# Moving router steps of a mixture-of-experts layer by one unit and by two tiles, in a kernel whose order is written out by hand

## The chip, the cores and the metric

The kernel runs on one core of a Trainium2 chip. The metric is the device time of one execution in microseconds (us). A core has the engines PE (matrix products), DVE, ACT and POOL, and SP, which here issues nearly all plain transfers. Each engine works through its own instruction list in order; semaphores hold an instruction until another engine or a transfer has got to a given point.

## The reference, cut to what matters

The reference is a two-layer decoder on 1024 tokens of width 128. The change touches the feed-forward part of its first layer, a mixture of 8 experts of which each token uses 2, applied twice ("loops"):

```python
for _ in range(LOOPS):                                  # LOOPS = 2
    z_norm = rmsnorm(z, norm_w)
    scores = softmax(z_norm @ router_w)                 # 8 experts
    topk_vals, topk_idx = top_k(scores, 2)
    topk_vals = topk_vals / (sum(topk_vals) + 1e-9)
    mixed = sum over e of cw[:, e] * ((silu(z_norm @ w1[e]) * (z_norm @ w3[e])) @ w2[e])
    z = mixed
x = x + z
```

Then follows the second layer, whose first part is a scan over the tokens (a state space layer).

## The kernel before

The 1024 tokens are two halves of 512. Two loops over two halves make four passes, 0 to 3. Passes 0 and 3 are **dense**: for all 512 tokens every expert is computed, in 16 **units** (an expert's 256 hidden columns are two units). PE makes two products per unit (`unit_up`, L1331), ACT the silu (`unit_silu`, L1339), DVE the product of both (`unit_gated`, L1345). Every second unit PE multiplies back (`down`, L1373), and DVE adds the result, weighted by the tokens' shares, to the sum in XN (`mix`, L1790). In the last pass the units are called n = 0 to 15 here; `down` number m = 8 follows unit n = 3 and uses units 0 and 1, `down` 9 follows unit 5 and uses units 2 and 3, and so on. `down` m waits until `mix` m-1 has read the PSUM bank that both use.

Passes 1 and 2 are **sorted**: each token's two (token, expert) pairs get a slot in a list of 15 tiles of 128 rows that is sorted by expert. POOL scatters the rows to HBM by eight indirect DMAs (`sort_tokens`, L2590), SP loads the sorted list back (`load_sorted`, L2623). Tile i goes through PE's first product (`tile_up`, L1440), ACT's silu (L1566), DVE's product (`tile_gated`, L1833), PE's transposes (`turn_tile`, L1449), ACT's copy (`take_hidden`, L1573) and PE's second product (`tile_down`, L1462). DVE copies each pair of results (L1842), SP stores them (`store_answers`, L2630), and POOL gathers each token's two rows again by eight indirect DMAs (`gather_answers`, L2600). The tiles of both sorted passes run as one loop, i = 0 to 29, after the units of pass 0 and before those of pass 3. At the end of the first 15 tiles PE drains: the last tiles are turned and multiplied one after the other, without new tiles between them.

**A pass's router** is a chain over three engines. PE turns the normed tokens (`pass_turn`, L1232), ACT copies them with the norm's weight (`pass_scalar`, L1512), PE multiplies by the router (`pass_logits`, L1238). DVE takes the logits and subtracts their maximum (`pass_shift`, L1660 to L1663), ranks each token's experts (`pass_rank`, L1672 to L1681), ACT takes the exponent (`pass_gates`, L1517), and DVE makes the shares (`pass_share`, L1688 to L1695). A sorted pass adds PE's counting (`pass_count`), DVE's slots (`pass_route`, up to L1716) and the expert of each tile (`pass_experts`). ACT's silu and its exponent are in different tables; each change between them is an ACT_TABLE_LOAD.

The order of all this on each engine is written out by hand: the loops of `experts_tensor`, `tiles_tensor`, `experts_scalar`, `tiles_scalar` and `experts_vector` insert a step after a given unit n or tile i. The router of pass 3 is inserted in the units of pass 3 itself. The router of pass 2 (`pass_turn(pe, 2)` and what follows) stands in the tile loop of pass 1, from tile 5 on. On SP the load of the second sorted list stands between the stores of pair 5 and pair 6 of the first; on POOL the first eight gathers stand behind the second eight scatters:

```python
sort_tokens(pool, 0); pass_power(pool, 0)
sort_tokens(pool, 1); gather_answers(pool, 0); pass_power(pool, 1)
def gather_answers(pool, k):
    pool.wait_ge(sig("answers_stored"), 16 * PAIRS * (k + 1))
    if k: pool.wait_ge(sig("mixed"), SORTED_MIXED)
```

After the units DVE and PE go on to the scan; its preparation for the first half (`scan_steps_in` and the like) stands inside the last units. In the middle of the last pass DVE adds the rows of the second eight gathers (`mix_choice`, L1740), makes the residual and its statistics (`half_residual`), ACT the root (`norm_root`, with a change of table) and DVE the norm (`half_norm`), which PE turns after unit 11 (`half_turn`).

Of the kernel before, what the change touches and what calls it, by code (L numbers as in the profile page):

```python
# [57 lines left out]
def build(nc, inp, out):  # L58
    ctx = ExitStack()
    with ctx:  # L60
# [1316 lines left out]
        def experts_tensor(pe):  # L1377

            for g in range(3, UPS):
                unit_up(pe, g)  # L1380
                if g % 2 == 1:
                    down(pe, (g - 3) // 2)
                if g == 5:
                    pass_turn(pe, 1)
                if g == 7:
                    pass_logits(pe, 1)
                if g == 8:
                    pass_count(pe, 0)
                if g in HALVES:
                    context_half_tensor(pe, HALVES.index(g))  # L1390
            tiles_tensor(pe)
            for g in range(UPS + 3, UNITS_MOE):
                n = g - UPS
                unit_up(pe, g)
                if g % 2 == 1:
                    down(pe, (g - 3) // 2)
                if n == 3:
                    pass_logits(pe, 3)
                if n == 11:
                    pe.wait_ge(sig("routed"), ROUTED["logits", 3])  # L1400
                    half_turn(pe, 0, 7)
                if n == 13:
                    scan_steps_in(pe, 0, SCAN_BANK[0][0])
                if n == 14:
                    scan_rows_in(pe, 0, SCAN_BANK[0][1])
                if n == 15:
                    scan_delta_in(pe, 0, SCAN_BANK[0][2])
            down(pe, UNITS_MOE // 2 - 1)

        def tiles_tensor(pe):  # L1410
# [58 lines left out]
            for i in range(TILES):  # L1469
                t = i % SLOT_TILES  # L1470
                tile_up(i)
                if t >= 2:
                    turn_tile(i - 2)
                if t >= 3:
                    tile_down(i - 3, starts[t - 3])
                if t % 4 == 1:
                    if load_of(i) % 4 < 3:
                        turn_sorted(load_of(i) + 1)
                if i == 5:
                    pass_turn(pe, 2)  # L1480
                if i == 7:
                    pass_logits(pe, 2)
                if i == 9:
                    pass_count(pe, 1)
                if i == SLOT_TILES - 1:
                    turn_tile(i - 1)
                    tile_down(i - 2, starts[t - 2])
                    turn_tile(i)
                    tile_down(i - 1, starts[t - 1])
                    tile_down(i, starts[t])  # L1490
                    starts = expert_starts(1)
                    keys_half_tensor(pe, 0)
                    turn_sorted(4)
                if i == SLOT_TILES:
                    keys_half_tensor(pe, 1)
                if i == SLOT_TILES + 1:
                    pe.wait_ge(sig("keys"), 2)
                    pe.wait_ge(sig("w_sums"), 1)
                    pe.matmul(bank(7)[:, 0:2], onesf, wscale[:, :], start=True, stop=True).then_inc(sig("w_total"), 1)
# [4 lines left out]
            tile_down(TILES - 1, starts[SLOT_TILES - 1])  # L1504
            pass_turn(pe, 3)
            unit_up(pe, UPS)
            unit_up(pe, UPS + 1)
            unit_up(pe, UPS + 2)

# [9 lines left out]
        def experts_scalar(act, ch):  # L1519
# [12 lines left out]
            for g in range(UPS, UNITS_MOE):  # L1532
                n = g - UPS
                unit_silu(act, g)
                if n == 2:
                    exp_and_ln(act)
                    pass_gates(act, 2)
                    pass_gates(act, 3)
                if n == 8:
                    exp_and_ln(act)  # L1540
                    norm_root(act, ch, 2, tiles_of(0))
                    act.wait_ge(sig("weights_in"), WEIGHTS)
                    act.activation(amat[:, :], amat[:, :], ACT.Exp).then_inc(sig("a_exp"), 1)
# [7 lines left out]
        def tiles_scalar(act):  # L1551
# [24 lines left out]
            for i in range(TILES):  # L1576
# [4 lines left out]
                if t % 4 == 2:  # L1581
                    if load_of(i) % 4 < 3:
                        take_sorted(load_of(i) + 1)
                if i == 6:
                    pass_scalar(act, 2)
                if i == SLOT_TILES - 1:
                    take_hidden(i - 1)
# [193 lines left out]
        def experts_vector(dve, ch):  # L1781
# [64 lines left out]
            for i in range(TILES):  # L1846
# [4 lines left out]
                    pass_stats(dve, ch, 2)  # L1851
                if i == 1:
                    pass_norm(dve, ch, 2)
                if i == 7:
                    pass_shift(dve, ch, 2)
                    pass_rank(dve, ch, 2)
                if i == 9:
                    pass_route(dve, ch, 1)
                if i == 10:
                    pass_experts(dve, ch, 1)  # L1860
                if i == 12:
                    feed_weight_sums(dve, ch)
# [16 lines left out]
            for g in range(UPS, UNITS_MOE):  # L1879
                n = g - UPS  # L1880
                unit_gated(dve, g)
                if n == 2:
                    pass_shift(dve, ch, 3)
                    pass_rank(dve, ch, 3)
                if n == 3:
                    pass_share(dve, ch, 3)
                if n >= 3 and g % 2 == 1:
                    mix((g - 3) // 2)
                if n == 4:
                    pass_share(dve, ch, 2)  # L1890
                    pass_pick(dve, ch, 1)
                if n == 7:
                    mix_choice(dve, ch, 1, 0)
                    mix_choice(dve, ch, 1, 1)
                    half_residual(dve, ch, 0)
                if n == 9:
                    half_norm(dve, ch, 0)
                if n == 11:
                    scan_constants(dve, ch)
# [969 lines left out]
```

## Time and profile before

| | |
|---|---|
| median of 3 runs | 589.55 us (589.21 to 591.85) |
| the profiled execution | 593.83 us, its span 592.1 us |
| PE busy | 495.4 us (84%) |
| DVE busy | 444.1 us (75%) |
| ACT busy | 278.8 us (47%) |
| POOL busy | 202.4 us (34%) |
| mean granted PE clock | 0.931 of full speed |

The span is what the trace covers; times in the rows count from its start. In a timeline row stand the start, the length, the engine, the line, the operation, what it writes and reads, and the count of instructions merged into it. A bracket gives the idle time of the engine ahead of it and what ended that; "issue" means that no wait is known, "remote" that the signal's sender could not be matched by time. PE's matmuls are pipelined and their ends are modelled. The tile loop and the last pass lie between 203 and 340 us of the span.

### The profile page before, as it was taken

How to read it: one execution, taken by the hardware profiler on the slowest of the kernel's cores; microseconds unless marked ns; L12 is line 12 of the kernel's file. 1: busy time of each engine (PE TensorE's matmuls, PEld its weight loads, DVE VectorE, ACT ScalarE, POOL GpSimd, SP SyncE). 2: the span in 40 equal slices, each digit the busy share in tenths (PEclk: the TensorE clock that was granted, in tenths of full speed). 3: DMA queues.
4: the chain of work that ended last, by engine and by line, in shares of the span. 5: the costliest groups of instructions: out<-in, count | busy, mean ns of one | idle time of the engine just before them, and what ended most of it. 6: DMA issues, size and time to landing. Idle time of an engine off the chain costs nothing.

```text
span 592.1 us, 9279 instructions
## 1 busy us (share of the span) xinstructions
PE 495.4 (84%) x3133; PEld 285.7 (48%) x3133; DVE 444.1 (75%) x1174; ACT 278.8 (47%) x519; POOL 202.4 (34%) x169
## 2 busy tenths in 40 slices
PE   7799899999989997698779944565579999999866
PEld 5344666666656665365456510121223666665423
DVE  7689866765775456056377779999999689998896
ACT  4631455555532243143314345645440377777555
POOL 8624000000005005311600015899994145554030
PEclk9899999999999999599979975788879999998989
DMA  5500340000101202311200000000000100000001
GB/s 135 159 16 1 119 131 2 2 1 3 45 1 35 68 19 66 107 41 45 71 2 0 2 1 0 0 0 1 0 1 10 36 2 1 3 2 2 1 1 37
DMA packets 25250, 17.28 MB, mean 29 GB/s; under 512 B 2962, under 2 KB 24020, under 8 KB 25204
## 3 DMA queue, kind: packets, MB, share of 16 engines
q1 hardware_dynamic: 24180, 14.59, 8.7%
q0 software_dynamic: 1024, 2.10, 1.1%
q8 instruction: 26, 0.43, 0.3%
q14 instruction: 20, 0.16, 0.1%
HBM read 10.00 MB, written 5.51 MB: 26 GB/s over the span
## 4 chain that ended last, share of the span: by engine, by line
PE 31%; DVE 23%; issue 8%; POOL 5%; ACT 3%; another core or an unknown queue 1%; DMA 1%; DVEq 0%; POOLq 0%; ACTq 0%
PE PS L1331 5%; PE PS L806 5%; DVE PS L2184 5%; DVE VA L2197 4%; PE PS L1373 4%; PE PS L851 3%; PE PS L868 3%; DVE PS L2190 2%; PE PS L1440 2%; POOL E L2142 1%; POOL OT L2600 1%; PE PS L1462 1%; DVE XN L1790 1%; POOL KSA L2134 1%
## 5 line engine op out<-in xcount | busy, mean ns | idle before, releaser
L851 PE MATMUL PS<-QM,KP 32*128 32x256 f32 x512 | 92.3, 400 | 1.2 <-ACT E L1039 0.8
L806 PE MATMUL PS<-KP,QP 32*128 32x256 f32 x512 | 78.0, 400 | 0.5 <-ACT QP L1017 0.5
L1039 ACT ACTIVATE E<-PS 128x512 f32<-128x512 f32 x100 | 56.1, 595 | 36.5 <-PE PS L851 24.2
L2590 POOL DMA_INDIRECT sorted<-VA,slot_of x16 | 15.7, 980 | 147.2 <-DVE expert_at L1724 127.1
L851 PEld LDWEIGHTS PS<-QM,KP 32*128 32x128 f32 x512 | 60.6, 184 | 6.2 <-issue 4.8
L356 PE MATMUL PS<-KSA,select 128*128 128x512 bf16 x64 | 25.7, 494 | 41.9 <-ACT KSA L2081 30.1
L1331 PE MATMUL PS<-XNT,KSA 128*128 128x512 f32 x128 | 59.2, 598 | 0.8 <-ACT XNT L1512 0.8
L806 PEld LDWEIGHTS PS<-KP,QP 32*128 32x128 f32 x512 | 51.3, 184 | 14.5 <-issue 10.1
L1114 DVE CUSTOM_DVE_ANT_0 SCR<-PS,KSA 128x256 f32<-128x256 f32 x128 | 47.5, 420 | 9.1 <-PE PS L806 8.3
L1109 DVE TENSOR_REDUCE MXT<-PS 128x2 f32<-128x512 f32 x64 | 41.1, 686 | 14.4 <-PE PS L806 14.4
L2565 POOL TENSOR_TENSOR VA<-VA,KSA 128x512 f32<-128x512 f32 x28 | 35.2, 1274 | 37.7 <-ACT VA L1044 37.7
L1339 ACT ACTIVATE E<-PS 128x512 f32<-128x512 f32 x32 | 18.8, 596 | 50.4 <-PE PS L1331 47.4
L1345 DVE TENSOR_TENSOR E<-E,PS 128x512 f32<-128x512 f32 x32 | 21.9, 686 | 27.5 <-ACT E L1339 22.2
L1373 PE MATMUL PS<-KSA,E 128*128 128x128 f32 x256 | 32.9, 284 | 9.4 <-DVE XN L1790 9.4
L1373 PEld LDWEIGHTS PS<-KSA,E 128*128 128x128 f32 x256 | 32.2, 199 | 17.8 <-issue 17.5
L2127 POOL TENSOR_SCALAR OT<-OT 128x1020 f32<-128x1020 f32 x16 | 16.7, 1042 | 62.2 <-ACT OT L2100 61.1
L2184 DVE TENSOR_TENSOR_SCAN PS<-OT,PS 128x1024 f32<-128x1024 f32 x16 | 36.7, 2295 | 1.4 <-ACT PS L2094 0.8
L2044 PE MATMUL PS<-E,ident 128*128 128x512 f32 x60 | 36.3, 738 | 1.0 <-POOL E L2142 1.0
L356 PEld LDWEIGHTS PS<-KSA,select 128*128 128x128 bf16 x64 | 5.0, 109 | 66.0 <-ACT KSA L2081 39.9
L2134 POOL TENSOR_TENSOR KSA<-SCR,KSA 128x1024 f32<-128x1024 f32 x15 | 35.2, 2347 | 4.8 <-ACT KSA L2081 4.8
L2142 POOL TENSOR_TENSOR E<-VA 128x1024 f32<-128x1024 f32 x15 | 35.2, 2348 | 2.9 <-PE PS L2044 2.0
L868 PE MATMUL PS<-E,VX 128*32 128x256 f32 x512 | 35.1, 393 | 0.1
(335 smaller groups left out, 1059.5 us busy)
## 6 DMA issues: line engine op xcount, KB each, us to landing
KSA<-in_w SPq DMA_DIRECT2D x2, 1024.0 KB, 6.9
sorted<-zeros SPq DMA_DIRECT2D x2, 960.0 KB, 6.4
answers<-OT SPq DMA_DIRECT2D x14, 128.0 KB
KSA<-in_w SPq DMA_DIRECT2D x2, 512.0 KB, 9.5
QP<-sorted SPq DMA_DIRECT2D x4, 256.0 KB, 3.1
QP<-sorted SPq DMA_DIRECT2D x2, 448.0 KB, 5.4
X<-in_x SPq DMA_DIRECT2D x2, 256.0 KB, 3.8
SCR<-in_ctxT SPq DMA_DIRECT2D x1, 512.0 KB, 6.0
```

The costliest lines, as they stand in the source:

```text
L806: ins = pe.matmul(score_bank(n, i)[:, q * S:(q + 1) * S], QP[rows(i), g, t:t + P], KP[rows(i), g, b * S:(b + 1) * S], start=True, stop=Tru ...
L851: ins = pe.matmul(o[:, kt * S:(kt + 1) * S], KP[rows(i), g, t:t + P], QM[rows(i), g, b * S:(b + 1) * S], start=True, stop=True, skip_group ...
L868: ins = pe.matmul(bank(6)[rows(i), (g % 2) * S:(g % 2) * S + S], VX[:, QT * b + kt, HG * g + i, :], slot(m, j)[:, kt * S:(kt + 1) * S], st ...
L1039: act.activation(slot(m, j), drain_bank(L, m, j), ACT.Exp).then_inc(sig("exps"), 1)
L1109: ins = dve.tensor_reduce(MXT[:, n % 2, :, c], o, AX, ALU.max, negate=True)
L1114: ins = dve.tensor_tensor_reduce(out=BIASED[:, i % 2, q, :], in0=o[:, q, :], in1=BIASQ[:, q, :], scale=-1.0, scalar=3e38, op0=ALU.add, op1 ...
L1331: ins = pe.matmul(unit_bank(g, o), w[:, e, c * P:(c + 1) * P], XNT[:, tokens_of(p)], start=True, stop=True)
L1373: ins = pe.matmul(bank(6)[:, t * P:(t + 1) * P], E6[:, (2 * m + c) % 4, t * P:(t + 1) * P], W2[:, m % NE, c, :], start=(c == 0), stop=(c = ...
L2044: ins = pe.matmul(bank(6 + half), ident[:, :], HC[n % 2][:, half * HALF:(half + 1) * HALF], start=(n == 0), stop=False, skip_group_check=True)
L2134: pool.tensor_tensor(DXB[n % 2], DX, BCOL[n % 2], ALU.mult).then_inc(sig("dxb"), 1)
L2142: pool.tensor_tensor(HC[n % 2], HH[n % 2], CCOL[n % 2], ALU.mult).then_inc(sig("outputs"), 1)
L2184: dve.tensor_tensor_scan(CARRY, DA[n % 3], FLOOR, 0.0, ALU.mult, ALU.add).then_inc(sig("carried"), 1)
```

## The change

Two blocks of steps are inserted at other places of the loops. No instruction is added or taken away.

In the last pass (units n): PE's `pass_logits(3)` goes from behind unit 3 and its `down` to between units 0 and 1. DVE's `pass_shift(3)` goes from after unit 2 to after unit 0, `pass_rank(3)` from 2 to 1, `pass_share(3)` from 3 to 2. ACT's `pass_gates` of passes 2 and 3, with the change of table, go from after unit 2 to after unit 1. Three later steps move the other way: DVE's choosing and residual from 7 to 8, ACT's root from 8 to 9, DVE's norm from 9 to 10.

In the tile loop: PE's `pass_turn(2)` goes from tile 5 to 4, `pass_logits(2)` from 7 to 5, `pass_count(1)` from 9 to 7; ACT's `pass_scalar(2)` from 6 to 4; DVE's shift and rank from 7 to 5, `pass_route(1)` from 9 to 7, `pass_experts(1)` from 10 to 8. The scatters of POOL and the load on SP are not moved in their lists; they wait for these steps.

The description of the change says as well that gathers wait only for their stores. The diff has no line on the gathers.

```diff
--- before.py
+++ after.py
@@ -1394,8 +1394,6 @@
                 unit_up(pe, g)
                 if g % 2 == 1:
                     down(pe, (g - 3) // 2)
-                if n == 3:
-                    pass_logits(pe, 3)
                 if n == 11:
                     pe.wait_ge(sig("routed"), ROUTED["logits", 3])
                     half_turn(pe, 0, 7)
@@ -1476,11 +1474,11 @@
                 if t % 4 == 1:
                     if load_of(i) % 4 < 3:
                         turn_sorted(load_of(i) + 1)
+                if i == 4:
+                    pass_turn(pe, 2)
                 if i == 5:
-                    pass_turn(pe, 2)
+                    pass_logits(pe, 2)
                 if i == 7:
-                    pass_logits(pe, 2)
-                if i == 9:
                     pass_count(pe, 1)
                 if i == SLOT_TILES - 1:
                     turn_tile(i - 1)
@@ -1504,6 +1502,7 @@
             tile_down(TILES - 1, starts[SLOT_TILES - 1])
             pass_turn(pe, 3)
             unit_up(pe, UPS)
+            pass_logits(pe, 3)
             unit_up(pe, UPS + 1)
             unit_up(pe, UPS + 2)
 
@@ -1532,11 +1531,11 @@
             for g in range(UPS, UNITS_MOE):
                 n = g - UPS
                 unit_silu(act, g)
-                if n == 2:
+                if n == 1:
                     exp_and_ln(act)
                     pass_gates(act, 2)
                     pass_gates(act, 3)
-                if n == 8:
+                if n == 9:
                     exp_and_ln(act)
                     norm_root(act, ch, 2, tiles_of(0))
                     act.wait_ge(sig("weights_in"), WEIGHTS)
@@ -1581,7 +1580,7 @@
                 if t % 4 == 2:
                     if load_of(i) % 4 < 3:
                         take_sorted(load_of(i) + 1)
-                if i == 6:
+                if i == 4:
                     pass_scalar(act, 2)
                 if i == SLOT_TILES - 1:
                     take_hidden(i - 1)
@@ -1851,12 +1850,12 @@
                     pass_stats(dve, ch, 2)
                 if i == 1:
                     pass_norm(dve, ch, 2)
-                if i == 7:
+                if i == 5:
                     pass_shift(dve, ch, 2)
                     pass_rank(dve, ch, 2)
-                if i == 9:
+                if i == 7:
                     pass_route(dve, ch, 1)
-                if i == 10:
+                if i == 8:
                     pass_experts(dve, ch, 1)
                 if i == 12:
                     feed_weight_sums(dve, ch)
@@ -1879,21 +1878,22 @@
             for g in range(UPS, UNITS_MOE):
                 n = g - UPS
                 unit_gated(dve, g)
+                if n == 0:
+                    pass_shift(dve, ch, 3)
+                if n == 1:
+                    pass_rank(dve, ch, 3)
                 if n == 2:
-                    pass_shift(dve, ch, 3)
-                    pass_rank(dve, ch, 3)
-                if n == 3:
                     pass_share(dve, ch, 3)
                 if n >= 3 and g % 2 == 1:
                     mix((g - 3) // 2)
                 if n == 4:
                     pass_share(dve, ch, 2)
                     pass_pick(dve, ch, 1)
-                if n == 7:
+                if n == 8:
                     mix_choice(dve, ch, 1, 0)
                     mix_choice(dve, ch, 1, 1)
                     half_residual(dve, ch, 0)
-                if n == 9:
+                if n == 10:
                     half_norm(dve, ch, 0)
                 if n == 11:
                     scan_constants(dve, ch)
```

## Rows read from the trace of the kernel before

**Rows 1.** Chain of waits, the piece after 285.9 us: start, length, what.
```profile
285.89 6.83 another core or an unknown queue
```

**Rows 2.** Busy time by stretch: length, PE, PEld, DVE, ACT, POOL, PE clock, DMA share, GB/s.
```profile
223.00:233.00 10.00, 9.30 (x60) 6.43 (x59) 7.68 (x29) 4.21 (x13) 4.87 (x5) 1.00 0.22 66
233.00:238.70 5.70, 1.15 (x9) 0.76 (x7) 0.85 (x2) 0.77 (x2) 2.87 (x3) 0.89 0.21 69
292.70:299.30 6.60, 0.00 (x0) 0.03 (x1) 6.03 (x23) 3.19 (x5) 0.37 (x1) 0.71 0.05 10
```

**Rows 3.** Timeline of PE in the last pass: start, length, instructions, idle before.
```profile
279.12 7.13 PE L1331 MATMUL PS<-XNT,KSA 128*128 128x512 f32 x16 [0.78 <-ACT XNT L1512]
286.09 1.95 PE L1373 MATMUL PS<-KSA,E 128*128 128x128 f32 x16
287.88 0.96 PE L1238 MATMUL PS<-router,XNT 128*128 128x8 f32 x8
288.69 3.68 PE L1331 MATMUL PS<-XNT,KSA 128*128 128x512 f32 x8
299.30 3.47 PE L1373 MATMUL PS<-KSA,E 128*128 128x128 f32 x16 [6.93 <-DVE XN L1790]
```

**Rows 4.** Timeline of DVE in the last pass.
```profile
281.77 0.69 DVE L1345 TENSOR_TENSOR E<-E,PS 128x512 f32<-128x512 f32 x1 [3.61 <-ACT E L1339]
292.75 0.19 DVE L1660 COPY logits<-PS 128x32 f32<-128x32 f32 x1 [6.86 <-remote]
293.31 0.42 DVE L1672 TENSOR_TENSOR VA<-logits 128x256 f32<-128x256 f32 x1
296.29 0.18 DVE L1688 TENSOR_REDUCE tok<-gates 128x4 f32<-128x32 f32 x1
298.03 1.13 DVE L1790 SCALAR_TENSOR_TENSOR XN<-PS,gates,XN 128x128 f32<-128x128 f32 x4
```

**Rows 5.** Timeline of ACT in the last pass.
```profile
285.19 1.28 ACT L258 ACT_TABLE_LOAD   x1
293.42 0.23 ACT L1517 ACTIVATE gates<-gates 128x32 f32<-128x32 f32 x1 [6.71 <-DVE gates L1663]
```

**Rows 6.** Timeline of POOL: first and last of the second eight gathers.
```profile
280.35 1.05 POOL L2600 DMA_INDIRECT OT<-answers,slot_of  x1 [4.24 <-DMA answers<-OT]
289.26 0.95 POOL L2600 DMA_INDIRECT OT<-answers,slot_of  x1 [0.30 <-issue]
```

**Rows 7.** Timeline of PE, tiles 12 to 14 of the first sorted pass.
```profile
226.81 1.02 PE L1440 MATMUL PS<-KSA,QM 128*128 x2
228.34 1.02 PE L1440 MATMUL PS<-KSA,QM 128*128 x2
232.25 0.41 PE L1449 MATMUL PS<-ident,QM 128*128 128x128 f32 x2 [0.70 <-issue]
235.81 0.41 PE L1449 MATMUL PS<-ident,QM 128*128 128x128 f32 x2 [2.62 <-issue]
238.67 1.22 PE L1462 MATMUL PS<-KSA,QM 128*128 x4 [1.93 <-ACT QM L1573]
```

**Rows 8.** Timeline of ACT at the end of these tiles.
```profile
235.28 0.38 ACT L1573 ACTIVATE QM<-PS 128x256 f32<-128x256 f32 x1 [3.18 <-remote]
238.15 0.38 ACT L1573 ACTIVATE QM<-PS 128x256 f32<-128x256 f32 x1 [2.48 <-remote]
```

**Rows 9.** Timeline of POOL: first and last of the second eight scatters.
```profile
226.75 1.03 POOL L2590 DMA_INDIRECT sorted<-VA,slot_of  x1 [15.80 <-DVE slot_of L1716]
235.67 0.96 POOL L2590 DMA_INDIRECT sorted<-VA,slot_of  x1 [0.30 <-issue]
```

**Rows 10.** Timeline of SP: the load of the sorted rows.
```profile
237.91 1.46 SPq L2623 DMA_DIRECT2D QP<-sorted  x3
```

**Rows 11.** Timeline of DVE: choosing the gathered rows.
```profile
309.07 2.31 DVE L1740 SCALAR_TENSOR_TENSOR XN<-OT,gate_of,XN 128x128 f32<-128x128 f32 x8
```

**Rows 12.** Timeline of PE: the down product after unit 11.
```profile
318.02 2.02 PE L1373 MATMUL PS<-KSA,E 128*128 128x128 f32 x16 [1.38 <-DVE XN L1790]
```

## Prediction, made before the changed kernel was run

> **What bounds the kernel now.** I read the chain of waits first, then busy time by stretch, then the timelines of the two stretches that the change touches. Over the whole span PE is the busiest engine, so a reader should look for places where PE stands still. In the chain the longest single piece inside the last pass is a wait of 6.83 us whose sender the trace does not know [rows 1]. The stretches show its effect: from 292.7 to 299.3 us PE does nothing, and DVE is busy for 6.03 of 6.60 us [rows 2]. A second hole lies at the end of the first sorted pass, where its tiles drain: from 233.0 to 238.7 PE works 1.15 of 5.70 us, 4.55 lost, while just before it was busy for 9.30 of 10 [rows 2].
>
> The first hole comes about so. PE makes the logits of the last pass behind unit 3 and `down` 8; they end at 288.84 [rows 3]. DVE starts on them only at 292.75, after 6.86 us of idling [rows 4]: their signal is 3.9 us late. In just this time POOL issues its last gathers; the eight run from 280.35 to 290.2 [rows 6]. ACT, whose list has the exponent behind unit 2's silu, stands for 6.7 us until 293.42 [rows 5]. Then DVE needs the shift (292.75 to 293.31, 0.6 us), the ranking with one gated product (293.31 to 296.29), and the shares (296.29 to 298.03, 1.7 us) before `mix` 8 (1.13 us) frees the bank for `down` 9 at 299.30 [rows 3, 4]. That product takes 3.47 us where `down` 8 takes 1.95 [rows 3]: the granted clock of the stretch ahead of it is 0.71, so that part of it was at 1.2 in place of 2.4 GHz [rows 2], after an engine that had stood for 6.9 us.
>
> The second hole has the same look. PE's transposes of tiles 13 and 14 end at 232.66 and 236.22 [rows 7]; ACT's copies that wait for them start at 235.28 and 238.15, 2.6 and 1.9 us later, with an unmatched sender [rows 8]. The other way the signal is prompt: the copy of 238.15 ends at 238.53 and PE starts at 238.67 [rows 7, 8]. POOL meanwhile issues eight scatters, 226.75 to 236.6 [rows 9]. So PE's signals reach others late toward the end of a batch of eight indirect DMAs; why, the trace does not say.
>
> **The last pass, part by part.** The same instructions, in another order; I lay out PE, DVE and ACT from PE's start at 279.12.
> Four units take 7.13 us less the overlap, 1.75 each [rows 3]. Logits cost PE 0.85 (287.88 to where unit 4 starts, 288.69) [rows 3] wherever they stand. Now: unit 0 to 281.1, logits to 282.0, units 1 to 3 to 283.7, 285.4 and 287.1, `down` 8 to 288.9, units 4 and 5 to 292.4, as before.
> DVE: product 0 ends at 282.46 [rows 4]; shift to 283.1, the logits being 0.5 us old; product 1 at 285.0; ranking, which is 2.98 less one product of 0.69, to 287.3 [rows 4].
> ACT: silu 1 ends at 284.3, table 1.28, two exponents of 0.23, table 1.28 [rows 5], 287.4, silu 2 (0.6) 288.0. The table change, which waited for DVE, now stands in front of silu 2, 2.0 us later than that unit's product; DVE's ranking covers 1.3 us of it.
> DVE then: product 2 to 288.7, shares to 290.4.
> Here the late signals decide. Unit 3 ends at 287.1, in the stretch, up to 292.7, in which rows 4 and 5 show nobody acting on a signal of PE. If it is held until 292.7: silu 3 293.3, product 3 294.0, `mix` 8 295.1, `down` 9 at 295.2, 4.1 us sooner than 299.30. If it is not held, product 3 is at 291.1, `mix` 8 at 292.2 and `down` 9 follows unit 5 at 292.4, 6.9 sooner. I take the held case, as its nearest row is a signal of PE held at this very place [rows 4]. PE then idles for 2.8 us in place of 6.9, and `down` 9 should come back from 3.47 toward 1.95: 1.5 more. Together 5.6 us (bounds: 4.1 with the slow clock kept, 8.4).
> What is late next: choosing and residual one unit later. Choosing starts at 309.07 [rows 11], 1.24 after unit 8 started; behind product 8 it starts some 3 us after it, 1.8 later. Before, PE waits 1.38 us ahead of `down` 12 for DVE [rows 12]. In the new order that wait shrinks, but PE's turning of the norm after unit 11 now waits for a norm that stands behind product 10. I give back 0.8 us (bounds 0 and 1.8). The gathers end long before. The scan's preparation and PE's filler keep their order and move along.
> The last pass: 5.6 - 0.8 = **4.8 us** gained (2.3 to 8.4).
>
> **The tile loop.** The block of steps is moved by two tiles nearly as a whole, and a tile is 1.53 us [rows 7]. PE, ACT and DVE have the same work to do, in a stretch in which PE has 9.30 busy of 10 us [rows 2], and each step keeps its distance, except that turning and logits are now one tile apart with ACT's copy between: cover 1.5 us for a copy of about 0.7, so nothing; without the cover PE waits up to 0.7. DVE's ranking at tile 5 delays the products of tiles 6 and 7, which PE turns two tiles later; at tile 7 it did so as well, and PE stood nowhere in that stretch. What is released sooner: POOL's scatters (some 223.6 in place of 226.75 [rows 9]), and behind them SP's load of the sorted rows (234.8 in place of 237.91 [rows 10]). Behind that load in SP's list stand the stores of pairs 6 and 7; pair 7's results are ready only after PE's last product of 238.67 [rows 7], so they win by PE alone. POOL's first gathers wait for those stores. I take it that PE does not wait for the load itself, which starts ahead of PE's last product of the pass.
> So the gain depends on where the late signals fall. They are seen from about 231.1 to 238.2, 7.1 us, and cost 4.55 [rows 2, 7, 8], 0.64 us per us. 3.1 us sooner, 3.1 of these 7.1 us fall on the steady loop. If they cost nothing there, the gain is 3.1 x 0.64 = 2.0; at the same rate it is 0; with three signals a tile in place of the drain's two it is a loss of 1.0. I take **1.0 us**, the middle between nothing lost and the same rate (bounds -1.0 and 4.55, the whole hole).
>
> **Sum.** 4.8 + 1.0 = 5.8 us of the profiled execution's 593.83. That execution is 4.3 us above the median of the runs, 589.55. I subtract from the median: **583.8 us**.
>
> **The rivals.**
> *The late signals belong to the recording, or are shorter in the timed runs.* For it: the profiled execution is 4.3 us longer, and the senders are unmatched exactly there. Against it: the holes sum to more than 4.3. Without late signals DVE would have had the logits at 288.9 before, and `down` 9 at some 295.4; new it is at 292.4, 3.0 sooner, less 0.8: 2.2 us, and nothing in the tile loop. **587.3 us**.
> The Trainium skill ("TensorE: Matmul & The Clock Gate", section "The cost: per-tile semaphore tail") gives 26.3 ns for each increment by a finished matmul, one after another. By that no signal would be microseconds late, and the time would be this rival's; the trace's 3.9 us [rows 3, 4] disagree.
> *The gathers are stretched.* DVE's shift, ranking and shares, 0.6 + 2.3 + 1.7 = 4.6 us, now run beside the second eight gathers, beside which DVE idled. If each us of them holds up POOL's issue, the gathers end at 294.8, and the late signals last until 297.3 in place of 292.7. Unit 3's silu then starts at 297.3, `mix` 8 ends at 299.8, and `down` 9 starts 0.5 us later than before, still at the slow clock; with 0.8 given back the pass loses 1.3, and with the tile loop's loss of 1.0 the kernel takes **591.9 us**. The pass gains nothing once the gathers end later than 293.5. Against it: the scatters beside a DVE busy for 7.68 of 10 us took 0.96 us [rows 2, 9], the gathers 0.95 [rows 6].
> The Trainium skill ("SBUF — State Buffer", the box on the trap "DVE blocks DMA") says that DVE in a 2-port mode locks GpSimd out while it writes descriptors, which speaks for this rival; the rows on the scatters do not show it.
> *The change does not do what it says, or both holes move rather than close.* The gathers' clause has no line in the diff, and the first gathers wait for a store already. If the drain is as long as before and the last pass is caught again by a root or table, the time is **589.5 us**.
> *Both holes close*: 8.4 + 4.55, **577 us**.
>
> **How the numbers follow.** Chances: forecast 0.50 (own range 581 to 586.5), shorter lateness 0.22, no move 0.12, stretched gathers 0.11, both closed 0.05. Measurement can tell 0.5%, 2.9 us, from no change: faster means under 586.6. Of the forecast 0.47 lies there, of the second 0.08, and the last 0.05: 0.60. Slower than 592.5 gets 0.04 of the fourth and 0.05 for prices that I did not see, which I take from the forecast and the second: 0.10, rounded up. Same 0.30. The range reaches from the better half of the gains to no move with some spread of runs: 578.5 to 590.5.
>
> **What would show it.** Right: DVE starts on the last logits within 1 us of their end near 282 of the old count; PE's hole ahead of `down` 9 is 3 us or less, and that product is at 2.4 GHz; scatters start 3 us sooner relative to tile 0; the drain loses less than 4.55. Wrong: gathers of over 1 us each, silu 3 held beyond 293, a new wait of PE ahead of the transposes of tiles 6 to 12, or both holes as long as before at other places.

## The result, and the profile after

The changed kernel takes 582.04 us (median of 4 runs, 580.10 to 583.49) against 589.38 us of the kernel before (4 runs, 587.01 to 591.85): a ratio of 0.987, 95% interval 0.9832 to 0.9909. Two later groups of runs of it gave 0.9894 [0.9856, 0.9932] and 0.9872 [0.9822, 0.9923]. Ratios compare fast runs alone: of the last group two of six, 587.40 and 589.51 us, were over 1.5% above the fastest and are left out of its ratio. The forecast was 583.8 us. It was close for reasons that were partly wrong, as the traces show.

PE's last pass in the changed kernel (timeline: start, length, instructions, idle before; answers to [rows 3]):

```profile
270.74 3.06 PE L1331 MATMUL PS<-XNT,KSA 128*128 128x512 f32 x4 [0.78 <-ACT XNT L1511]
273.60 1.72 PE L1238 MATMUL PS<-router,XNT 128*128 128x8 f32 x8
275.17 6.96 PE L1331 MATMUL PS<-XNT,KSA 128*128 128x512 f32 x12
283.75 3.60 PE L1331 MATMUL PS<-XNT,KSA 128*128 128x512 f32 x8
287.41 2.02 PE L1373 MATMUL PS<-KSA,E 128*128 128x128 f32 x16
```

`down` 9, the last line, follows unit 5 with no idle time named before it, at the full 2.4 GHz: 2.02 us in place of 3.47. The 6.93 us in which PE stood are gone. But unit 0 and the logits are slow: 3.06 and 1.72 us. The stretches of the changed kernel show why (length, PE, PEld, DVE, ACT, POOL, PE clock, DMA share, GB/s; answers to [rows 2]):

```profile
227.60:233.30 5.70, 5.49 (x33) 3.85 (x32) 3.14 (x7) 2.43 (x8) 4.48 (x5) 1.00 0.28 89
270.70:280.80 10.10, 10.06 (x22) 5.29 (x23) 2.66 (x8) 2.63 (x5) 6.79 (x7) 0.66 0.35 101
280.80:287.40 6.60, 6.55 (x28) 3.59 (x27) 6.19 (x19) 3.17 (x7) 3.89 (x2) 1.00 0.12 32
```

The first line is the stretch up to the end of the drain of the first sorted pass: PE works 5.49 of 5.70 us where the profiled execution of before had 1.15. The change did not bring this about: a second profile of the kernel before (e1 below) has 5.48 of 5.70 us there. The third line is the stretch ahead of `down` 9: 6.55 of 6.60 us where the profiled execution had 0.00. The second, which holds units 0 to 2 and the start of unit 3, has a mean clock of 0.66.

DVE and ACT of the changed kernel answer to [rows 4, 5]:

```profile
275.35 0.19 DVE L1659 COPY logits<-PS 128x32 f32<-128x32 f32 x1 [0.19 <-PE PS L1238]
282.13 1.03 DVE L1680 TENSOR_SCALAR chosen<-place 128x32 f32<-128x32 f32 x1
286.14 1.12 DVE L1789 SCALAR_TENSOR_TENSOR XN<-PS,gates,XN 128x128 f32<-128x128 f32 x4
```

```profile
279.35 1.28 ACT L258 ACT_TABLE_LOAD   x1
280.64 0.35 ACT L1516 ACTIVATE gates<-gates 128x32 f32<-128x32 f32 x2
```

DVE takes the logits as soon as PE has made them, ACT's exponents find their input ready, and `mix` 8 ends before unit 5 does. The scatters start at 223.65, 17.58 us after PE's first tile product (206.07); in the second trace of before (e1 below) it is 20.63 (207.88 to 228.51). So they are 3.05 us sooner, two tiles, as forecast. The first scatter, e1 first, then changed:

```profile
228.51 1.03 POOL L2590 DMA_INDIRECT sorted<-VA,slot_of  x1 [15.80 <-DVE slot_of L1716]
```

```profile
223.65 1.03 POOL L2590 DMA_INDIRECT sorted<-VA,slot_of  x1 [12.74 <-DVE slot_of L1715]
```

In the changed kernel's trace no engine waits for a sender that the trace doesn't know. So all four signs of being right that the prediction had named came true. They do not tell its held signals from its first rival, under which no signal is late.

### The profile page after: what moved, and what is told of

Read it like the earlier page. It is cut to its first block, busy times and chain, and to the rows that moved or that the text cites. A ratio compares the mean times of both kernels' runs of the same rounds, so it can differ in the third digit from the quotient of the medians.

```text
span 578.4 us, 9279 instructions
## 1 busy us (share of the span) xinstructions
PE 492.7 (85%) x3133; PEld 284.3 (49%) x3133; DVE 444.4 (77%) x1174; ACT 278.8 (48%) x519; POOL 202.7 (35%) x169
## 4 chain that ended last, share of the span: by engine, by line
PE 31%; DVE 23%; issue 6%; POOL 6%; ACT 3%; DMA 1%; SPq 0%; DVEq 0%; POOLq 0%; ACTq 0%
PE PS L1331 7%; PE PS L806 5%; DVE PS L2184 5%; DVE VA L2197 4%; PE PS L1373 3%; PE PS L851 3%; PE PS L868 3%; DVE PS L2190 2%; POOL E L2142 2%; POOL OT L2600 1%; POOL sorted L2590 1%; POOL KSA L2134 1%; PE PS L2044 1%; PE PS L826 1%; DMA answers<-OT 1%
## 5 line engine op out<-in xcount | busy, mean ns | idle before, releaser
L1331 PE MATMUL PS<-XNT,KSA 128*128 128x512 f32 x128 | 62.0, 621 | 0.8 <-ACT XNT L1511 0.8
L1373 PEld LDWEIGHTS PS<-KSA,E 128*128 128x128 f32 x256 | 30.8, 192 | 10.2 <-issue 9.9
L1331 PEld LDWEIGHTS PS<-XNT,KSA 128*128 128x128 f32 x128 | 23.4, 197 | 24.1 <-issue 22.8
```

The lines of the kernel that those rows point to most:

```text
L1331: ins = pe.matmul(unit_bank(g, o), w[:, e, c * P:(c + 1) * P], XNT[:, tokens_of(p)], start=True, stop=True)
L1373: ins = pe.matmul(bank(6)[:, t * P:(t + 1) * P], E6[:, (2 * m + c) % 4, t * P:(t + 1) * P], W2[:, m % NE, c, :], start=(c == 0), stop=(c = ...
```

## The experiments

A trace without the late signals is called undisturbed here. "Half clock" is PE at 1.2 GHz, a granted clock of 0.50 in the rows, "full clock" 2.4 GHz, 1.00. Marks that several experiments use are starts of groups in PE's timeline: the first tile product of the first sorted pass, the end of its drain, the first tile product of the second, unit 0, `down` 9, the two turnings of the norm, and, in DVE's timeline, the first scan.

**e1, the kernel before, once more.** No edit.

> The kernel before, unchanged, once more. Theory A (the late signals of PE belong to this order of the steps): the profile shows them again, DVE starts on the last logits over 3 us after PE has made them, and PE works under 2 us between the drain's start and its last product; ratio 1.00 within 0.005. Theory B (they come and go from execution to execution, whatever the order): this profile may be without them, and its span is then some 8 to 10 us shorter than the first one's 592.1.

589.19 us, 0.9995 [0.9965, 1.0025]. Its trace (span 587.3 us) has none of the late signals on which the forecast was built, as Theory B allowed; but the span is 4.8 us shorter, not 8 to 10. PE and DVE at the end of the last pass:

```profile
275.79 8.83 PE L1331 MATMUL PS<-XNT,KSA 128*128 128x512 f32 x16 [0.78 <-ACT XNT L1512]
286.24 0.96 PE L1238 MATMUL PS<-router,XNT 128*128 128x8 f32 x8
293.96 3.75 PE L1373 MATMUL PS<-KSA,E 128*128 128x128 f32 x16 [3.23 <-DVE XN L1790]
```

```profile
287.24 0.19 DVE L1660 COPY logits<-PS 128x32 f32<-128x32 f32 x1 [2.98 <-PE PS L1238]
290.35 0.69 DVE L1345 TENSOR_TENSOR E<-E,PS 128x512 f32<-128x512 f32 x1
292.69 1.13 DVE L1790 SCALAR_TENSOR_TENSOR XN<-PS,gates,XN 128x128 f32<-128x128 f32 x4
```

DVE has the logits at once, and PE's hole is 3.23 us in place of 6.93. It is DVE's own work: shift, ranking, product, shares and mix, 6.72 us from 287.24 to 293.96, against 3.68 us that PE has to do in units 4 and 5. At the end of the drain the copies wait for nobody unknown (window 229.3 to 235.0 us); PE stands further on:

```profile
229.30:235.00 5.70, 5.48 (x33) 3.87 (x32) 3.86 (x10) 2.44 (x8) 4.17 (x6) 1.00 0.34 103
```

```profile
234.72 1.43 PE L1462 MATMUL PS<-KSA,QM 128*128 x8
239.48 2.05 PE L390 MATMUL PS<-SCR,wx 128*128 128x512 f32 x2 [3.33 <-issue]
242.47 1.11 PE L1421 MATMUL PS<-ident,QP 128*128 128x128 f32 x4 [0.95 <-DMA QP<-sorted]
```

First 3.33 us that the profile calls issue: PE fetches the second pass's expert numbers into registers there. Then 0.95 us for the load of the sorted rows, of which the forecast had said that PE doesn't wait for it. Its first part is issued at 239.66 and lands 2.8 us later, at 242.46; PE starts at 242.47. What follows the fetch runs at half clock (window 238.4 to 248.6 us of the same trace):

```profile
238.40:248.60 10.20, 7.32 (x11) 3.05 (x12) 0.42 (x1) 2.10 (x4) 1.96 (x2) 0.50 0.44 129
```

**e2, the tile loop's part alone.**

```diff
# PE; ACT's scalar and DVE's steps of the third pass alike
-                if i == 7:
+                if i == 5:
                     pass_logits(pe, 2)
```

> The tile loop's block moved, the last pass as before. Theory A: the drain of the first sorted pass loses its hole of 4.55 us in every execution, 3 to 5 us faster than before, and DVE still gets the last logits late. Theory B: 0 to 1 us, as the third pass's slots are not what PE waits for. My prediction had 1.0 us (-1.0 to 4.55).

587.83 us, 0.9938 [0.9908, 0.9968]: some 0.6% or 3.6 us, the size that Theory A gave, but not from its hole. From the first tile product to the end of the drain takes 28.40 us, as in e1 (28.27): the drain is not where the gain is. It lies behind it:

```profile
237.54 2.04 PE L390 MATMUL PS<-SCR,wx 128*128 128x512 f32 x2 [3.25 <-issue]
239.38 1.06 PE L1421 MATMUL PS<-ident,QP 128*128 128x128 f32 x4
241.30 1.12 PE L1440 MATMUL PS<-KSA,QM 128*128 x2 [0.86 <-ACT QM L1559]
```

The wait for the load is gone, the fetch of 3.25 us is left, and the clock comes back at 240.7:

```profile
237.30:240.70 3.40, 2.90 (x6) 1.39 (x6) 0.00 (x0) 0.91 (x2) 0.00 (x0) 0.50 0.78 221
240.70:271.30 30.60, 27.61 (x141) 17.99 (x142) 17.64 (x59) 13.45 (x36) 9.48 (x10) 1.00 0.18 51
```

**e3, the last pass's part alone**: every hunk of the change that e2 leaves out.

```diff
             unit_up(pe, UPS)
+            pass_logits(pe, 3)
# with the shift, ranking, shares, exponents, and choosing, root and norm, as in the change
```

> The last pass's steps moved, the tile loop as before. Theory A: 4 to 6 us faster than before, the hole of the drain stays at over 4 us. Theory B: 2 to 3 us faster, which is what the order gives without late signals. My prediction had 4.8 us (2.3 to 8.4).

583.94 us, 0.9902 [0.987, 0.9934]. From unit 0 to `down` 9 takes 15.48 us in place of e1's 18.17, and `down` 9 runs at full clock. PE's hole ahead of it has shrunk from 3.23 to 0.53 us:

```profile
291.38 2.02 PE L1373 MATMUL PS<-KSA,E 128*128 128x128 f32 x16 [0.53 <-DVE XN L1789]
```

By the ratio that is some 5.8 us, Theory A's size again, though no signal is late in this trace. It comes from 2.69 us up to `down` 9, 1.73 in it, 0.28 up to the first turning of the norm and 1.60 behind the second. The gains of the two parts, 0.6% and 1.0%, add to more than the whole's 1.1 to 1.3%, within their intervals.

**e4, the changed kernel again.** No edit.

> The changed kernel, unchanged, once more. Theory A: no late signal in the profile, as in the first one, and a ratio of 0.983 to 0.991 to the kernel before. Theory B: late signals may show now, at the scatters under tiles 10 to 14 or at the second gathers, with a span above 582 us.

583.53 us, 0.9894 [0.9856, 0.9932], and no late signal: Theory A. From the first tile product to DVE's first scan takes 134.72 us, in the first trace of it 134.73: this part of the kernel repeats to a hundredth where the clock does.

**e5, the tile loop's block moved by one tile in place of two.**

```diff
-                if i == 7:
+                if i == 6:
                     pass_logits(pe, 2)
```

> The kernel before with the tile loop's block moved by one tile only (turning 5 to 4, logits 7 to 6, counting 9 to 8, and so on), so that the scatters and the load start some 1.5 us sooner in place of 3. Theory L (PE waits for the load of the sorted rows, 0.95 us in the second trace of before): 1.5 us are enough, and the gain is that of two tiles, 3 to 4 us (ratio about 0.994). Theory S (what counts is how far the scatters are from the drain): about half of it, 1.5 to 2 us.

585.40 us, 0.9922 [0.9888, 0.9956]: the same as e2 within the intervals, so one tile is enough (Theory L). PE no longer waits for the load, and only the fetch is left:

```profile
239.69 2.05 PE L390 MATMUL PS<-SCR,wx 128*128 128x512 f32 x2 [3.24 <-issue]
241.53 1.06 PE L1421 MATMUL PS<-ident,QP 128*128 128x128 f32 x4
```

Half clock lasted 10.2 us here all the same (238.8 to 249.0), so its length is not set by that wait alone.

**e6 and e7, the key's product ahead of the fetch**, in the kernel before (e6) and in the changed one (e7).

```diff
-                    starts = expert_starts(1)
                     keys_half_tensor(pe, 0)
+                    starts = expert_starts(1)
```

> The kernel before, with the first half of the keys' product, 2 us of PE at the low clock, put ahead of the load of PE's registers instead of behind it, so that it runs while the registers load. Theory L: PE only gets to the transposes of the sorted rows sooner and waits there for the same load: the wait grows from 0.95 by 1 to 2 us, and the time is the same within 0.7 us. Theory S: nothing holds PE there, and it is 1 to 2 us faster.

> The changed kernel with the same move of the keys' product. Theory L: here the load has landed by then, so the 1 to 2 us are gained, 575 to 577 us of span in a trace whose span was 578.4, and a ratio to the kernel before of 0.985 to 0.988. Theory S: the same as the changed kernel.

e6: 589.72 us, 0.9985 [0.9955, 1.0015], no gain. e7: 580.16 us, 0.9819 [0.9785, 0.9854]. PE's next turning, e6 first:

```profile
245.68 1.12 PE L1421 MATMUL PS<-ident,QP 128*128 128x128 f32 x4 [5.47 <-DMA QP<-sorted]
```

```profile
240.40 0.63 PE L1419 MATMUL PS<-ident,QP 128*128 128x128 f32 x4 [2.96 <-DMA QP<-sorted]
```

From the end of the drain to the first tile product takes 8.31 us in e6 as in e1 (8.30): the load sets the pace there, and what PE does sooner turns into waiting. In the changed order it takes 5.31 us in e7 against 6.99. The bracket names the load there too, but the load is issued at 236.94 and lands 2.8 us later, at 239.74, 0.66 us before PE starts; in e6 PE starts 0.02 us after the landing. What is left for PE to wait for is the fetch, whose end the profile does not show.

These 1.68 us are not a gain of e7's trace, though. In it the half clock of 3.4 us falls behind the first tile product of the second sorted pass (241.89), from 242.4 to 245.9, and not ahead of it. The second half of the key's product takes 1.91 us there, 1.02 in the changed kernel:

```profile
241.89 1.59 PE L1438 MATMUL PS<-KSA,QM 128*128 x2 [0.86 <-ACT QM L1558]
243.27 1.91 PE L390 MATMUL PS<-SCR,wx 128*128 128x512 f32 x2
244.98 1.45 PE L1438 MATMUL PS<-KSA,QM 128*128 x2
```

From that product to the turning of the last pass e7 takes 29.55 us against 27.86. Counted from the first tile product of the first sorted pass, it is level with the changed kernel by that turning (63.25 us against 63.24). What it is ahead by at DVE's first scan, 1.18 us, comes from units 0 to 3, where half clock lasted 3.4 us in place of 6.8. Its span, 579.2 us, is not the 575 to 577 that Theory L gave either. So e6 shows that in the old order PE waits for the load; that e7's shorter median comes from the fetch is argued and not shown.

**e8, the changed kernel with PE kept at work ahead of unit 0**: eight products that nobody reads.

```diff
+            fill(5)     # five products of the identity into bank 0
             pass_turn(pe, 3)
+            fill(3)
             unit_up(pe, UPS)
```

> The changed kernel with products that nobody reads on PE where it stands ahead of the last pass: five 128x512 bf16 ones before the turning, three behind it. Theory C (the half clock over the first units, 6.8 us of it in the trace of the changed kernel, is what makes both parts together gain less than their sum): unit 0 takes some 1.9 us in place of 3.1, and the kernel is 1.2 to 2.5 us faster than the changed kernel, ratio to before 0.985 to 0.988. Rival: the clock is low there in any case, or ACT and DVE set the pace; no faster than the changed kernel.

580.89 us, 0.9834 [0.9798, 0.987]: better than the changed kernel's 0.987 to 0.9894, but the intervals overlap. In the trace the half clock within units 0 to 3 is gone:

```profile
272.24 1.24 PE L1467 MATMUL PS<-identb 128*128 128x512 bf16 x5
274.14 0.81 PE L1467 MATMUL PS<-identb 128*128 128x512 bf16 x3
275.08 1.98 PE L1331 MATMUL PS<-XNT,KSA 128*128 128x512 f32 x4
276.90 0.95 PE L1238 MATMUL PS<-router,XNT 128*128 128x8 f32 x8
277.71 5.40 PE L1331 MATMUL PS<-XNT,KSA 128*128 128x512 f32 x12
```

From unit 0 to `down` 9 takes 13.11 us in place of 16.67. The products lie in PE's wait for DVE and ACT around the turning, which takes as long as before (1.44 us to unit 0, against 1.43). The changed kernel without them stands twice there, 1.24 us for DVE and the 0.78 shown above ahead of unit 0:

```profile
269.31 0.66 PE L1232 MATMUL PS<-ident,VA 128*128 128x128 f32 x4 [1.24 <-DVE VA L1651]
```

So these 2.0 us of standing cost 3.6 us more by the slow clock behind them in this trace. In e3 and e7, which stand there alike but have half clock for only 3.4 us, up to `down` 9 takes 15.48 and 15.47 us, 2.4 more than here.

**e9, e7 and e8 together; e10, the same with four more such products between the key's product and the fetch.**

```diff
                     keys_half_tensor(pe, 0)
+                    fill(4)     # e10 alone
                     starts = expert_starts(1)
```

> The changed kernel with both additions of the two runs ahead: the keys' product in front of the register load, and eight products that nobody reads around the last turning. Theory C (the half clock behind the drain and the wait for the sorted rows are two separate costs, each with its own cover): the gains add. Filled, the changed kernel stood at 0.983 of the kernel before; with the keys first at 0.982; the changed kernel itself at 0.987 and 0.989. Adding the two gives 0.977 to 0.979, some 576 us. In the trace unit 0 takes 1.98 us and PE's wait for the sorted rows stays near 3 us. Rival: both additions close the same hole (the one shortens the standing ahead of the units, the other bridges it), so the sum is no better than either: 0.981 to 0.984.

> The same, and four more unread products on PE between the keys' product and the register load. Theory C: they take about 0.9 us of a wait of 3 us for the sorted rows and cost nothing, and if they keep the clock over the drain the remaining half-clock stretch of 3.4 us there shrinks, worth up to 1.7 us: 0.975 to 0.978. Rival: the register load that follows stands for some 3.2 us whatever is ahead of it, so the products only delay it, 0.9 us later: 0.979 to 0.981, not better than without them.

e9: 577.69 us, 0.9829 [0.98, 0.9857]. e10: 578.14 us, 0.9832 [0.9805, 0.9859]. e9 has the lowest median of all versions and e7 the lowest ratio; none of the four can be told from the others. Theory C said that the gains add; e9's ratio lies in its rival's range (0.981 to 0.984), and its interval leaves 0.977 to 0.979 out. The traces point the same way. The eight products do their part in both: unit 0 takes 1.98 us. The key's product ahead of the fetch brings nothing in e9's trace: from the first tile product of the first sorted pass to the last turning it takes 63.87 us against the changed kernel's 63.24, with half clock from 238.5 to 245.3. As in e7, then, no gain of it is left ahead of the units, and at the units the eight products have already removed the slow clock. In e10 no half clock is left behind the drain, the turning of the sorted rows starts 3.67 us after it in place of e9's 3.33, and 61.42 us remain of the 63.24:

```profile
234.20:240.00 5.80, 2.99 (x13) 1.25 (x12) 0.29 (x1) 1.38 (x2) 0.00 (x0) 1.00 0.67 194
```

But 1.55 us go again behind the second turning of the norm, at half clock in this trace, and in time e10 brings nothing that can be measured: its ratio is above both ranges that were expected of it.

**e11, choosing, root and norm put back by one unit**, and **e12, the changed kernel beside it**, no edit.

```diff
-                if n == 8:
+                if n == 7:
                     mix_choice(dve, ch, 1, 0)
# the root (9 to 8) and the norm (10 to 9) alike
```

> The changed kernel with choosing, the root and the norm put back by one unit, where they stood in the kernel before; all else as changed. The prediction gave 0.8 us back for this move (0 to 1.8). If that stands, the time is 0.8 us under the changed kernel: a ratio about 0.0014 lower than it (0.986 to 0.988), with PE's wait ahead of the half's turning (1.38 us) shorter. Rival: choosing one unit earlier again stands in front of the product that a mix waits for, and PE's wait ahead of down 12 grows from 0.7 to 1.4 us or more while the half's turning gains less: no difference, or up to 1 us slower, 0.988 to 0.991.

> The changed kernel unaltered, as the mark for the three others on the same chip: 0.987 to 0.990 of the kernel before. All theories expect no signal of PE later than 1 us at either place; a late one here would say that the changed order can have them too, and that the disturbed execution of the kernel before was not a property of its order.

e11: 583.70 us, 0.9897 [0.986, 0.9935]; e12: 584.94 us, 0.9872 [0.9822, 0.9923], its runs from 576.98 to 589.51 us. In e12 no signal is late. The times tell nothing of a term of 0.8 us. The traces do, e11 first, then e12 (the `down` product behind unit 11, and the turning of the norm):

```profile
309.27 2.02 PE L1373 MATMUL PS<-KSA,E 128*128 128x128 f32 x16 [1.38 <-DVE XN L1789]
311.13 0.60 PE L1773 MATMUL PS<-ident,XN 128*128 128x128 f32 x4
```

```profile
309.10 2.02 PE L1373 MATMUL PS<-KSA,E 128*128 128x128 f32 x16 [0.67 <-DVE XN L1789]
312.50 0.63 PE L1773 MATMUL PS<-ident,XN 128*128 128x128 f32 x4 [1.38 <-DVE XN L1766]
```

From the end of `down` 9 to the turning takes 17.11 us in e11 and 17.95 in e12: moving this block later costs 0.84 us.

## Why the prediction came out as it did

**Where the gain comes from.** The undisturbed trace of before (e1) against the changed kernel's first one, by the marks, in us:

| stretch | e1 | changed | saved |
|---|---|---|---|
| end of the drain to the next tile product | 8.30 | 6.99 | 1.31 |
| from there to the turning of the last pass | 29.91 | 27.86 | 2.05 |
| unit 0 to `down` 9 | 18.17 | 16.67 | 1.50 |
| `down` 9 itself | 3.75 | 2.02 | 1.73 |
| to the first turning of the norm | 18.22 | 17.95 | 0.27 |
| second turning to DVE's first scan | 11.98 | 10.38 | 1.60 |

With the other stretches, of which the drain alone differs by as much as 0.12, that is 8.31 of 143.04 us. Of the two spans' difference, 587.3 - 578.4 = 8.9, the rest is 1.8 won ahead of the first tile product and 1.2 lost behind the first scan, where the change does nothing.

**How much of it is the clock.** Each timed execution has a span and a mean granted clock. Of before 68 have a mean span of 588.08 us at 0.9258; of the changed kernel 14 (two left out, as above) have 580.91 us at 0.9360. One line through both, shifted between them, falls by 2.9 us for each 0.01 of clock. So of 7.2 us some 2.9 go with the clock and 4.3 are left at the same clock. That the clock's share comes from the waits of PE that the change closes fits the marks above and e8; for the timed executions, of which only the mean clock is known, it is argued and not shown.

**The last pass: sum right, main step wrong.** Forecast 4.8 us; measured 1.50 + 1.73 + 0.27 + 1.60 = 5.1. That the sums agree is luck: the hole, forecast at 4.1, gave 1.50, and 1.60 came from a place that the forecast did not have.
The step that failed is "Here the late signals decide", with the hole of 6.9 us cut by 4.1 to 2.8. The held signal was an accident of the one profiled execution: of 14 profiles none of the other 13 has an engine waiting between 200 and 310 us for a sender that the trace doesn't know. The timed executions bear that out. By the line of the 68, a span at that execution's clock of 0.931 is 586.6 us; it took 592.1, 5.5 above, where the 68 scatter about it with a standard deviation of 1.1 and at most 2.9. In its place stands what the first rival had: DVE's chain from logits to `mix` 8, 6.5 us by its working (288.9 to 295.4) and 6.72 in e1. The edit takes it off PE's path, but for 0.53 us in e3 and e7, so unit 3's signal held until 292.7 and the remaining hole of 2.8 us failed with it.
Right were `down` 9's clock (1.5 forecast, 1.73 measured), DVE taking the logits at once, and the give-back by choosing, root and norm (0.8 forecast, 0.84 in e11 against e12). It is hidden in the 0.27 saved above, since in e1 half clock lasted until 299.8 and cost 1.1 of that stretch: at full clock it is 17.10 us before (e2) and 17.95 after. A small slip of reading, 0.85 us of PE for the logits where the rows give 0.81 (287.88 to 288.69), changes nothing.
Missing were two terms of the clock. Within units 0 to 3 half clock lasts 6.8 us in the changed kernel and 3.4 in e1, which takes 1.2 of the 2.69 us that e3 saves up to `down` 9. And the small products behind the second turning run at full clock in the changed kernel, at half in e1. So it is in all five traces with the old last pass, and of the nine with the new one only e10 has half clock there; why, no run tested. One of these products, e1 first, then changed:

```profile
341.86 1.94 PE L1949 MATMUL PS<-XNT,wssm 128*32 128x512 f32 x8
```

```profile
332.83 1.06 PE L1949 MATMUL PS<-XNT,wssm 128*32 128x512 f32 x8
```

**The tile loop: right in what moves, wrong in why it pays.** Forecast 1.0 us, measured 1.31 + 2.05 - 0.12 (up to the drain) = 3.2, inside the bounds. The scatters come 3.05 us sooner, and no new wait of PE appeared. The step that failed is "I take it that PE does not wait for the load itself, which starts ahead of PE's last product of the pass": that held only because the drain was stretched by 5.5 us in the disturbed execution (33.79 us against 28.27 in e1). In e1 the load starts at 239.66, behind the drain's end at 236.15, and PE waits; in the changed kernel it starts at 234.81, lands 2.6 us later, and PE comes to it only at 239.53, behind the fetch and the key's product. SP's load, e1 first, then changed:

```profile
239.66 1.46 SPq L2623 DMA_DIRECT2D QP<-sorted  x3
```

```profile
234.81 1.46 SPq L2623 DMA_DIRECT2D QP<-sorted  x3
```

The sizing by the share of late signals that falls on the loop has nothing under it. Of the 3.2 us the 2.05 are clock and not certain in each execution: the half clock behind the drain lasted 10.2 or 10.3 us in all three undisturbed traces with the old tile loop (e1, e3, e6), and 3.4 or 3.5 in e2 and the changed kernel's three, but 10.2 in e5, whose block is moved by one tile, and 10.3 in e11, whose tile loop is the changed one. In e11 the stretch of the 2.05 us took 30.50 us, longer than e1's 29.91.

**The rivals.** The first (lateness belongs to the recording) had the right mechanism and the wrong price: its 587.3 left out the half clock behind the hole, the load, and the clock in the loop. Its 2.2 us for the last pass were the hole alone, 3.0, less the give-back. The Trainium skill ("TensorE: Matmul & The Clock Gate", section "The cost: per-tile semaphore tail"), beside which it stood, gives 26.3 ns for each increment; the 13 undisturbed profiles agree in that no signal is late by microseconds, and do not resolve the figure. The stretched gathers are refuted at the size that was given: the eight take 0.95 to 1.10 us each in the changed kernel and end at 282.01, 11.27 us after unit 0, where e1's end at 286.89, 11.10 after. One of the eight takes 1.02 to 1.15 us in every trace of the new order, where those of the old order take 0.95 to 0.97 behind the first; what stretches it was not tested. The Trainium skill ("SBUF — State Buffer", the box on the trap "DVE blocks DMA") speaks of DVE holding GpSimd's descriptors up; no run here shows that as the cause. Nor did the holes merely move. "Both holes close" at 577 is what the traces look like, but the larger half of both holes was not in the timed runs.

**What stays open.** It is open why one execution had signals of PE late by microseconds beside the gathers and scatters; no run tested it. Nor is it known why the half clock behind the drain lasts 3.4 us in e12 and 10.3 in e11, whose instructions up to there are the same (e12 first, then e11):

```profile
242.50:245.90 3.40, 2.90 (x6) 1.39 (x6) 0.00 (x0) 0.84 (x2) 0.00 (x0) 0.50 0.79 228
```

```profile
238.50:248.80 10.30, 8.30 (x13) 3.59 (x14) 0.42 (x1) 2.45 (x4) 4.09 (x5) 0.50 0.43 122
```

## What to carry to other kernels

Before a step is built on a long wait whose sender the trace doesn't know, compare the profiled execution's time with the timed runs, at the same granted clock: here it lay 5.5 us above their line, and a second profile would have halved the hole. The time alone is not enough: two later executions of the same kernel took 594.0 us, at a mean clock of 0.913 and within 1 us of the line. A pause of PE of 2 to 3 us is to be priced with the slow products behind it, here another 2.4 to 3.6 us. Work put ahead of a late load pays nothing (e6). And a stretch that became shorter is no gain until the one behind it has been measured: e7's 1.68 us were gone 30 us later, as the slow clock had only moved.

## What the runs showed of the hardware that was not expected

Products that nobody reads can pay: eight of them, 2.05 us of PE in a pause, saved 3.56 us up to `down` 9 in the trace by removing the half clock (e8). In the timed runs the gain over the changed kernel is not clear of the noise.

A fetch of expert numbers into PE's registers held the engine for 3.2 to 3.3 us, shown only as issue (e1, e2, e5 and the changed kernel). Behind the key's product it is put down to the load, which in e7 had landed 0.66 us before PE went on.

A small DVE instruction was stretched where POOL's large TENSOR_SCALAR began: DVE's L1680 took 1.03 us in four traces (the changed kernel's three and e11), in the changed kernel's first from 282.13, 0.05 us behind POOL's start; the same instruction took 0.18 us in e1. POOL in the changed kernel:

```profile
280.91 1.10 POOL L2600 DMA_INDIRECT OT<-answers,slot_of  x1 [0.30 <-issue]
282.08 2.79 POOL L2745 TENSOR_SCALAR OT<-SCR 128x1024 f32<-128x1024 uint8 x1
```

In e3 and e7, where another instruction of DVE stands at this place (L1689), that one took 0.86 and 0.87 us in place of 0.19, and in e1, e2, e5 and e6 L1663 took 0.37 to 0.43 in place of 0.19. In all ten traces the stretched instruction ends 1.08 or 1.09 us after POOL's start, wherever it began itself, while other small ones of DVE beside the same POOL instruction took their usual time (L1660 and L1662 in e1: 0.19 us each). In e3 and e7 L1689 stands on the chain to `mix` 8, and they are the only two traces of the new order with a hole ahead of `down` 9, 0.53 us. No run moved POOL's instruction to test it.
